# Making a mixer's cross-chunk term from C-B blocks instead of a state, with the decays exponentiated in PSUM

## The reference, cut to what matters

```python
xch = (hs * dt[..., None]).reshape(b, nc, CHUNK, H, P)
A_cum = jnp.cumsum(A_dt, axis=-1)
L = jnp.exp(_segsum(A_dt))                       # decay from s to l inside a chunk
Y_diag = jnp.einsum('bzlhn,bzshn,bhzls,bzshp->bzlhp', Cc, Bc, L, xch)
decay_states = jnp.exp(A_cum[..., -1:] - A_cum)
states = jnp.einsum('bzlhn,bhzl,bzlhp->bzhpn', Bc, decay_states, xch)
...
Y_off = jnp.einsum('bzlhn,bzhpn,bhzl->bzlhp', Cc, prev, jnp.exp(A_cum))
Y = (Y_diag + Y_off).reshape(b, s, H, P) + hs * D[None, None, :, None]
g = y * jax.nn.silu(gate)
```

## Time and profile before

| | us |
|---|---|
| median of 3 runs | 2859.91 |
| lowest and highest | 2858.87, 2861.09 |
| the profiled execution's own time | 2862.66 |
| its span, first to last instruction | 2860.9 |

### The profile page before, as it was taken

One profiled execution on the slowest core, in us unless ns is written; L12 is line 12 of the kernel. 1 busy time (PEld: TensorE's weight loads), 2 busy tenths in 40 slices (PEclk: granted clock), 3 DMA queues, 4 the chain that ended last, 5 costly groups with the idle time before them and its releaser, 6 DMA issues. The chain is left out here.

```text
span 2860.9 us, 47552 instructions
## 1 busy us (share of the span) xinstructions
PE 2699.3 (94%) x13630; PEld 2171.6 (76%) x13630; DVE 1977.7 (69%) x2745; ACT 1395.8 (49%) x2545; POOL 1519.4 (53%) x1420
## 2 busy tenths in 40 slices
PE   4999999999998597999999999999999999999979
PEld 3778778778776375877877777777778777788767
DVE  5675675666665697587677677677777676776864
ACT  3433433433433444565565565546646546655621
POOL 1654654654653044575575575566566565665710
PEclk8999999999999698999999999999999999999999
DMA  2011011011010132101101001010010111011011
GB/s 89 19 53 34 18 52 34 22 49 38 22 38 14 52 128 83 36 27 47 39 31 55 31 32 48 31 50 29 32 56 29 39 47 32 31 47 39 9 49 45
DMA packets 72621, 118.32 MB, mean 41 GB/s; under 512 B 10310, under 2 KB 22214, under 8 KB 72373
## 3 DMA queue, kind: packets, MB, share of 16 engines
q1 hardware_dynamic: 72388, 115.61, 12.1%
HBM read 102.92 MB, written 12.65 MB: 40 GB/s over the span
## 5 line engine op out<-in xcount | busy, mean ns | idle before, releaser
L1490 DVE TENSOR_TENSOR mx_m<-mx_ex,mx_CBM 128x512 f32<-128x512 f32 x256 | 295.5, 1176 | 138.0 <-ACT mx_ex L1413 135.4
L221 PE MATMUL proj<-slab_hi,XTL 128*128 128x512 f32 x832 | 362.3, 435 | 5.5 <-DVE ad_gate L1668 5.5
L221 PE MATMUL proj<-XTH,slab_lo 128*128 128x512 f32 x736 | 299.3, 407 | 39.3 <-PEq L81 18.4
L204 DVE TENSOR_TENSOR slab_lo<-slab_raw,slab_hi 128x512 fp32r<-128x512 f32 (+2 forms) x272 | 236.9, 884 | 143.8 <-ACT slab_hi L195 119.8
L223 PE MATMUL proj<-slab_hi,XTH 128*128 128x512 f32 x832 | 327.6, 394 | 0.0
L222 PE MATMUL proj<-slab_lo,XTH 128*128 128x512 f32 x832 | 324.9, 390 | 0.0
L223 PE MATMUL proj<-XTH,slab_hi 128*128 128x512 f32 x736 | 291.0, 395 | 0.0
L222 PE MATMUL proj<-XTL,slab_hi 128*128 128x512 f32 x736 | 290.8, 395 | 0.0
L1552 POOL TENSOR_TENSOR mx_gate<-mx_gate,mx_hd 128x512 f32<-128x512 f32 x128 | 176.5, 1379 | 157.7 <-DVE mx_hd L1477 146.6
L1278 PE MATMUL core_y<-mx_xch,mx_m 128*128 128x64 f32 x2048 | 243.3, 272 | 0.0
L1278 PEld LDWEIGHTS core_y<-mx_xch,mx_m 128*128 128x128 f32 x2048 | 240.0, 192 | 1.5
(11 more groups left out here) (313 smaller groups left out, 6894.9 us busy)
## 6 DMA issues: line engine op xcount, KB each, us to landing
slab_raw<-in_w_gate SPq DMA_DIRECT2D x64, 256.0 KB, 3.1
slab_raw<-in_w_out SPq DMA_DIRECT2D x64, 256.0 KB, 3.1
slab_raw<-in_w_x SPq DMA_DIRECT2D x60, 256.0 KB, 3.9
slab_raw<-in_w_q SPq DMA_DIRECT2D x32, 256.0 KB, 3.1
slab_raw<-in_w_g SPq DMA_DIRECT2D x32, 256.0 KB, 3.1
slab_raw<-in_w_o SPq DMA_DIRECT2D x32, 256.0 KB, 3.0
bc_scratch<-bc_acc SPq DMA_DIRECT2D x32, 256.0 KB, 2.0
slab_raw<-in_w_bc SPq DMA_DIRECT2D x20, 256.0 KB, 4.5
```

The source lines that it names most:

```text
L204: op = nc.vector.tensor_tensor(K.SL[par][:, c, 0:width], K.RAW[c][:, 0:width], hi, ALU.subtract)
L221: nc.tensor.matmul(to[:, 0:bh.shape[-1]], al, bh, start=(c == 0), stop=False)
L1490: nc.vector.tensor_tensor(M[(2 * t + k) % 4][:, :, :], EX[k][:, :, :], CBM[:, t:t + 1, :].broadcast_to([P, 4, P]), ALU.mult).then_inc(S["m ...
```

## The change

- BK, ST, the state matmul of even tiles (line 1284) and ScalarE's copy (line 1403) go. In BK's place CBO holds, for each sequence, the block B (first chunk) times C (second chunk), made by four f32 matmuls in place of the four transposes. For odd tiles one matmul CBO times XD gives what C times ST gave.
- GpSimd waits with XD for the output product of the odd tile (`mx_pof`) of the sequence before, where it waited for the state matmul (`mx_o`).
- Relu and Exp work in place in the decay banks. EX goes. VectorE reads the banks for M. TensorE's decay matmul, and the input unit 1 that uses PD[1], wait for M (`mx_m`) where they waited for Exp (`mx_e`); ScalarE's wait for M goes.

```diff
-        BK = sb("BK", [P, NB, N1])
+        CBO = sb("CBO", [P, NB, P])
...
-        EX = [sb(f"ex{i}", [P, 4, P]) for i in range(2)]
...
-                if t % 2 == 0:
+                if t % 2:
                     pe.wait_ge(S["mx_xd"], HEAD + NB * q + b + 1)
                     pe.wait_ge(S["mx_to"], HEAD + NB * q + b)
-                    nc.tensor.matmul(K.PO[:, :], BK[:, b, :], XD[:, :, :], start=True, stop=True).then_inc(S["mx_o"], 1)
-                else:
-                    pe.wait_ge(S["mx_st"], HEAD + NB * q + b + 1)
-                    nc.tensor.matmul(K.PO[:, :], CT[:, t * P:(t + 1) * P], ST[:, :], start=True, stop=True).then_inc(S["mx_pof"], 1)
+                    nc.tensor.matmul(K.PO[:, :], CBO[:, b, :], XD[:, :, :], start=True, stop=True).then_inc(S["mx_pof"], 1)
...
                         for b in range(NB):
-                            tr = nc.tensor.transpose(K.PO[:, b * P:(b + 1) * P], BT[:, 2 * b * P:(2 * b + 1) * P], K.ident[:, :])
-                        tr.then_inc(S["mx_a"], 1)
+                            mm = nc.tensor.matmul(K.PO[:, b * P:(b + 1) * P], BT[:, 2 * b * P:(2 * b + 1) * P],
+                                                  CT[:, (2 * b + 1) * P:(2 * b + 2) * P], start=True, stop=True)
+                        mm.then_inc(S["mx_a"], 1)
...
                         for k in range(2):
-                            pe.wait_ge(S["mx_e"], HEAD + 16 * q + 2 * t + k - 1)
+                            pe.wait_ge(S["mx_m"], HEAD + 16 * q + 2 * t + k - 1)
...
                     elif sl == 1:
-                        pe.wait_ge(S["mx_e"], HEAD + 16 * q)
+                        pe.wait_ge(S["mx_m"], HEAD + 16 * q)
...
-                    if r in YSLOT and YSLOT.index(r) % 2 == 0:
-                        b = YSLOT.index(r) // 2
-                        act.wait_ge(S["mx_o"], HEAD + NB * q + b + 1)
-                        nc.scalar.activation(ST[:, :], K.PO[:, :], ACT.Copy).then_inc(S["mx_st"], 1)
...
                             act.wait_ge(S["mx_d"], HEAD + 16 * q + 2 * t + k + 1)
-                            act.wait_ge(S["mx_m"], HEAD + 16 * q + 2 * t + k - 1)
-                            ex = EX[k][:, :, :].rearrange("p h n -> p (h n)")
-
-                            nc.scalar.activation(ex, PD[k][:, :], ACT.Relu, scale=-1.0).then_inc(S["mx_rl"], 1)
+                            nc.scalar.activation(PD[k][:, :], PD[k][:, :], ACT.Relu, scale=-1.0).then_inc(S["mx_rl"], 1)
                             act.wait_ge(S["mx_rl"], HEAD + 16 * q + 2 * t + k + 1)
-                            nc.scalar.activation(ex, ex, ACT.Exp, scale=-1.0).then_inc(S["mx_e"], 1)
+                            nc.scalar.activation(PD[k][:, :], PD[k][:, :], ACT.Exp, scale=-1.0).then_inc(S["mx_e"], 1)
...
-                            nc.vector.tensor_tensor(M[(2 * t + k) % 4][:, :, :], EX[k][:, :, :],
+                            nc.vector.tensor_tensor(M[(2 * t + k) % 4][:, :, :], PD[k][:, :].rearrange("p (h n) -> p h n", h=4),
                                                     CBM[:, t:t + 1, :].broadcast_to([P, 4, P]), ALU.mult).then_inc(S["mx_m"], 1)
...
                             pool.wait_ge(S["mx_xc"], HEAD + NT * q + t + 1)
-                            pool.wait_ge(S["mx_o"], HEAD + NB * q + b)
+                            pool.wait_ge(S["mx_pof"], HEAD + NB * q + b)
```

More of the change, by code:

```diff
@@ L172 @@
     + ["bc_ld", "bc_a", "bc_tap", "bc_th", "bc_p", "bc_cm", "bc_st0", "bc_st1", "bc_st2", "bc_st3"]
-    + ["mx_ld", "mx_zero", "mx_set", "mx_bc", "mx_row0", "mx_row1", "mx_a", "mx_tap", "mx_th", "mx_cm", "mx_hsT", "mx_pt", "mx_hs", "mx_o",
-       "mx_pof", "mx_cb", "mx_bt", "mx_d", "mx_e", "mx_m", "mx_xc", "mx_hd", "mx_xd", "mx_y", "mx_yb", "mx_st",
+    + ["mx_ld", "mx_zero", "mx_set", "mx_bc", "mx_row0", "mx_row1", "mx_a", "mx_tap", "mx_th", "mx_cm", "mx_hsT", "mx_pt", "mx_hs",
+       "mx_pof", "mx_cb", "mx_bt", "mx_d", "mx_e", "mx_m", "mx_xc", "mx_hd", "mx_xd", "mx_y", "mx_yb",
        "mx_to", "mx_gth", "mx_gate", "mx_q", "mx_rs", "mx_acc0", "mx_acc1", "mx_x", "mx_p", "mx_sum", "mx_rl"]
@@ L1202, in mixer_phase @@
         CBM = sb("CBM", [P, NT, P])
-        BK = sb("BK", [P, NB, N1])
+        CBO = sb("CBO", [P, NB, P])
         acc = [sb(f"acc{i}", [P, HALF]) for i in range(3)]
         th = sb("th", [P, HALF])
-        EX = [sb(f"ex{i}", [P, 4, P]) for i in range(2)]
         M = [sb(f"m{i}", [P, 4, P]) for i in range(4)]
         XCH = [sb(f"xch{i}", [P, HH1, P1]) for i in range(2)]
-        XD, TO, ST = sb("xd", [P, HH1, P1]), sb("to", [P, HW]), sb("st", [P, HW])
+        XD, TO = sb("xd", [P, HH1, P1]), sb("to", [P, HW])
         HD = [sb(f"hd{i}", [P, HW]) for i in range(2)]
@@ L1398, in half @@
                         act.wait_ge(S["mx_a"], HEAD + 3 * g + 3)
-                        nc.scalar.activation(BK[:, :, :].rearrange("p b n -> p (b n)"), K.PO[:, :], ACT.Copy).then_inc(S["mx_bt"], 1)
-                    if r in YSLOT and YSLOT.index(r) % 2 == 0:
-                        b = YSLOT.index(r) // 2
-                        act.wait_ge(S["mx_o"], HEAD + NB * q + b + 1)
-                        nc.scalar.activation(ST[:, :], K.PO[:, :], ACT.Copy).then_inc(S["mx_st"], 1)
+                        nc.scalar.activation(CBO[:, :, :].rearrange("p b n -> p (b n)"), K.PO[:, :], ACT.Copy).then_inc(S["mx_bt"], 1)
                     if r in SCORE1:
```

## The result

| | kernel before | changed kernel |
|---|---|---|
| median of 4 runs each, us | 2860.5 | 2808.84 |
| lowest and highest | 2858.87, 2864.54 | 2805.85, 2812.59 |
| the profiled execution's own time | 2862.66 | 2805.85 |
| its span | 2860.9 | 2804.1 |

The ratio is 0.9818, with a 95% interval of 0.9801 to 0.9835: 51.7 us faster between the medians, where 52.8 had been forecast. Later groups of five runs of the same kernel gave 0.9821 (0.9808 to 0.9835) and 0.9808 (0.9793 to 0.9824), 50.1 and 54.4 us between the medians.

The account below looks back on a forecast made before the run. The prediction took TensorE's full queue as the bound: -58.2 us for removed matmuls, +3.0 for blocks, +2.4 for new waits, together -52.8 us, from 2859.91 to 2807.1 us. Forecast 2802 to 2814 us (0.68), wider range 2799 to 2828.

Parts of the forecast that it names:

- The bound: Over the mixer TensorE runs at its own rate, so a matmul removed from its queue comes off the time.
- 0.91 us per matmul: TensorE's queue: each of 64 removed BK state matmuls saves 0.91 us start to start, 58.2 us in all.
- +3.0 us for the blocks: On TensorE, C-B blocks take 0.82 us where transposes took 0.44, eight times: 3.0 us more.
- Wait 1: TensorE's decay matmul waits for VectorE's mask product; tightest at tile 2, margin 0.05 us; all three waits 2.4 us.
- Wait 2: GpSimd's XD waits for the odd tile's output product; margins 0.4 us before tiles 5 and 7 in second halves.
- Rival a: GpSimd's chain behind XD decides: stretched operations delay tiles 5 and 7 in second halves, 18 us, 2825 us; chance 0.17.
- Wait 3: VectorE in slot 11: tile 7's product comes earlier and needs HD of tile 6; about even, priced at 0.15 us.
- Rival b: The in-place chain through PSUM is slower; gain gone if 2.1 us longer, 2880 us at 2.5; chance 0.04.
- Rival c: The removed matmul was hidden anyway and input units' waits grow instead: about 2855 to 2862 us; chance 0.04.
- Rival d: Input units' waits on ScalarE and GpSimd shrink or clock drops vanish: up to 8 us more, 2799 us; chance 0.07.
- What the trace would show: Decay matmul intervals: tile 1 to 2 near 3.8 us, 0 to 1 from 10.0 to 9.1, half from 50.16 to 47.4.

Follow-up runs that it names:

- double product: The changed kernel with the odd tile's output matmul issued twice, 64 f32 matmuls more: 2859.19 us, ratio 1.000 to the kernel before.
- two XD buffers: The kernel with the C-B blocks alone (decays still through SBUF), given two XD buffers in turn instead of one: 2810.51 us, ratio 0.9836.
- the longer chain: The changed kernel with a third activation, a Relu that changes nothing, between Relu and Exp in both decay banks: 2850.49 us, ratio 0.9959.
- after_a: A later trace of the changed kernel, run again unchanged as the measure for the kernels beside it: 2809.57 us, ratio 0.9821.
- after: The first profiled execution of the changed kernel, compared with the kernel before: 2805.85 us, the fastest of its four runs.
- state_only: Against the changed kernel, decays go the old way through SBUF, so only the C-B blocks replace the state: 2822.73 us, ratio 0.9867.
- psum_only: Against the kernel before, decays in place in PSUM and mask product out of PSUM, state matmul and copy kept: 2861.21 us, ratio 1.0004.

## Why the prediction was right, step by step

The predicted 2807.1 us stands against 2808.84, and -52.8 us against -51.7 between the medians (-50.1 and -54.4 in the later groups); in the profiled executions it was -56.8.

- **The bound.** Right. TensorE's queue sets the time: taking out 64 matmuls gave it, putting 64 in took it back (double product), and relieving VectorE by 122 us without touching TensorE gave nothing (decays in place alone).
- **0.91 us per matmul.** Right: the intervals 3-4 and 5-6 shrank by 0.91 and 0.92 us, and 7-0 of first halves by 0.93. In second halves the last interval shrank by 0.18 only: less 0.45 for the blocks that stand in it, less 0.35 by a longer wait on VectorE's low part (0.54 instead of 0.19 us at the turn of tile 7), which leaves 0.11; the rest is within the scatter.
- **+3.0 us for the blocks.** Too small as a size, and not paid on balance. The prediction read 0.82 us from blocks with a projection unit behind them; with the decay matmul behind them they take 0.90, so it is 8 x 0.45 = 3.6 us. They took the place of a wait on ScalarE's copy in slot 2, which the earlier trace rows had in its total and which I had called unchanged. That interval fell by 1.44 us in first halves, not 0.91. Turning the blocks back brought the wait back.
- **Wait 1.** Priced near zero and was. The margin was 0.05 in the sum and about 0.25 us in the trace. The chain to the end of the mask product took 3.44 us, not 3.48, and that already has the signal to VectorE in it, for which the sum added another 0.14; the decay matmul came 0.04 us later.
- **Wait 2.** XD does wait for the product (0.59 us at tile 6), but TensorE doesn't, and for the reason that was given: with the mask products out of PSUM, GpSimd's operations behind XD keep their short lengths. The run of the blocks alone showed the same wait where that cover is missing, at 0.86 us, tile 7, second halves; at tile 5 it did not come. Rival a, priced at 18 us, has at most the 13 us that kernel lacks; two XD buffers gave back 9.
- **Wait 3.** Expected in slot 11 at 0.15 us. No wait there; it came three slots later (14) and only in second halves, 0.35 us more than before, 2.5 us in seven. That this is near the 2.4 that all three were to cost is luck.
- **Rival b** had the wrong price, as the longer chain showed: the work queued behind it was left out.
- **Rival c** is ruled out by the same two kernels as show the bound.
- **Rival d**, at 0.07, came true in part: the waits on ScalarE's copies shrank by 2.9 us, and the clock drop of the earlier trace rows is missing in this trace of the changed kernel. But `after_a` has two such drops, so the change didn't take them away.
- **What the trace would show:** 47.4 us from first to last decay matmul was 46.92 and 47.30; 9.1 from tile 0 to 1 was 8.57 and 8.96; 3.8 at tile 2 was 3.85.

Trace against trace the forecast was 4 us short, and one miss makes it: the interval from tile 0 to tile 1, which lost 0.53 us more than the product in first halves and 0.07 in second ones, 4.8 us in all, as the wait in slot 2 went. Against the medians it was 1 us off. That is closer than the executions allow, some 10 us from lowest to highest and gains of 50.1 to 54.4 us in three groups, so it is partly luck. Of the 7.4 us between the traces `after` and `after_a`, 4.1 lie in the last interval of second halves, and the two drops of the clock make some 3 of them (an estimate, from 55.1 and 55.5 us against 53.8 at most elsewhere in these traces). What sets the rest of the scatter stays open.

## What to carry to other kernels

Where one engine's queue is full, price a removed instruction from start to start in that queue, and then read every place where it stands: here 56 of 64 were worth the full 0.91 us, and in the other eight a wait on VectorE took back about a third of it. An edit that relieves other engines may be worth nothing alone and still be what lets the first one have its gain: the in-place decays gave 0 us alone and 13 us beside the blocks, 9 of which a second XD buffer gives as well. When a chain gets longer, price also what is queued behind it on its engine; and before a cost is added next to a wait, ask whether it only fills the wait.

## What was not expected of the hardware

Relu of 128 x 512 f32 out of PSUM took 0.598 and 0.582 us (the two banks) into SBUF, and 0.582 and 0.578 in place. Exp took 0.632 us from SBUF to SBUF and 0.582 in PSUM. This agrees with the Trainium skill (ScalarE: Activation LUTs, Step-by-step: what each stage is for), where PSUM is called the faster destination; for Relu, where only the destination changed, it is by 0.016 and 0.004 us.

The mask product took 0.673 to 0.693 us with a PSUM source, with a median of 0.691, and from SBUF 0.675 at the least. The Trainium skill (VectorE: DVE Perf Modes, the section on the TRN2 errata) gives a PSUM source 62 cycles more of fixed term, 0.065 us; no such step shows here, and the measurement decides. With two SBUF inputs the product's median was 1.166 us and its longest 1.786, and GpSimd's product for HD had a median of 1.49 us in `state_only` and 1.04 in the changed kernel. Moving one input to PSUM alone (`psum_only`) took 122 us off VectorE and 72 off GpSimd.

An f32 matmul of 512 columns costs 0.91 us behind head products but 0.86 behind its like. Four f32 blocks of 128 columns cost 0.81 us to a projection unit behind them and 0.90 to a decay matmul.
